# Streaming pairs of 256-token chunks as 512 columns past each weight block in a two-layer conditioned transformer block

## The reference

```
# layer 0
x = x + modulated_rms_norm(attention_16_heads(x, mask) @ Wo.T)
# layer 1, its norms with gain and bias from the condition
x = x + attention_16_heads(norm1(x)) @ Wo.T
x = x + (silu(norm2(x) @ gate_w.T) * (norm2(x) @ hid_w.T)) @ out_w.T   # 256 -> 1024 -> 256
```

## Time and profile before

| | |
|---|---|
| median of 3 runs | 324.24 us (323.45 to 324.27) |
| profiled execution: span | 321.4 us |
| its own time | not given apart from the span; the median is 2.8 us above it |
| TensorE busy | 314.3 us (98%), 5016 matmuls |
| VectorE, ScalarE, GpSimd busy | 239.0, 204.5, 182.0 us |
| transfers | 17.08 MB, mean 53 GB/s |
| mean duration of a 256-column matmul in feed-forward | 282 to 285 ns |

### The profile page before, as it was taken

One profiled execution on the slowest core, in us unless ns is written; L12 is line 12 of the kernel. 1 busy time (PEld: TensorE's weight loads), 2 busy tenths in 40 slices (PEclk: granted clock), 3 DMA queues, 4 the chain that ended last, 5 costly groups with the idle time before them and its releaser, 6 DMA issues.

```text
span 321.4 us, 11942 instructions
## 1 busy us (share of the span) xinstructions
PE 314.3 (98%) x5016; PEld 297.9 (93%) x5016; DVE 239.0 (74%) x425; ACT 204.5 (64%) x445; POOL 182.0 (57%) x207
## 2 busy tenths in 40 slices
PE   7999999999999999999999999999999999999996
PEld 7979978899999999999989999998999999999996
DVE  4995879896996987896949498898953783554344
ACT  4897687899874687587575765685462466333231
POOL 7499797244667366478742757478380653453310
PEclk9998999999999999999999999999999999999999
DMA  7955731304000300310004000100000100000001
GB/s 238 303 170 179 237 104 35 102 4 134 2 3 2 100 2 2 103 36 0 4 2 134 0 6 0 37 0 5 2 1 2 36 33 2 2 11 24 2 33 36
DMA packets 11238, 17.08 MB, mean 53 GB/s; under 512 B 1328, under 2 KB 5440, under 8 KB 11184
## 3 DMA queue, kind: packets, MB, share of 16 engines
q1 hardware_dynamic: 11008, 15.80, 15.6%
q0 software_dynamic: 176, 0.51, 0.8%
HBM read 14.14 MB, written 2.16 MB: 51 GB/s over the span
## 4 chain that ended last, share of the span: by engine, by line
PE 82%; DVE 6%; POOL 4%; issue 4%; ACT 2%; DMA 1%; SPq 0%; DVEq 0%; POOLq 0%; ACTq 0%
PE ps L1594 63%; PE ps L1709 6%; PE ps L1691 5%; PE ps L1742 3%; PE ps L1778 2%; PE ps L1727 2%; DVE probs L1148 1%; PE ps L1679 1%; DVE row_max L1140 1%; POOL x L442 1%; DMA x_T<-in_xT 1%; POOL w_lo L411 1%; POOL x_row L422 1%; DVE xs_g L1215 1%; DVE xs_row L1202 1%
## 5 line engine op out<-in xcount | busy, mean ns | idle before, releaser
L474 POOL TENSOR_TENSOR h_lo<-w_stage,h_hi 128x512 fp32r<-128x512 f32 x29 | 37.4, 1290 | 43.0 <-ACT h_hi L769 43.0
L468 POOL TENSOR_TENSOR probs<-probs,inv_row 128x512 f32<-128x512 f32 x40 | 41.3, 1050 | 34.3 <-DVE inv_row L1161 34.2
L1140 DVE TENSOR_REDUCE row_max<-ps 128x8 f32<-128x512 f32 x64 | 40.8, 681 | 9.6 <-PE ps L1691 9.4
L706 ACT ACTIVATE probs<-probs 128x512 f32<-128x512 f32 x64 | 38.8, 633 | 9.6 <-DVE probs L1148 9.3
L1234 DVE SCALAR_TENSOR_TENSOR w_stage<-w_stage,ps 128x512 f32<-128x512 f32 x32 | 21.7, 677 | 29.9 <-ACT w_stage L762 29.8
L1148 DVE SCALAR_TENSOR_TENSOR probs<-row_max,ps 128x512 f32<-128x512 f32 x64 | 41.1, 677 | 0.9 <-PE ps L1709 0.9
L1594 PE MATMUL ps<-ff_hi,w_hi 128*128 128x256 f32 x256 | 41.6, 285 | 0.0
L1594 PE MATMUL ps<-ff_lo,w_hi 128*128 128x256 f32 x256 | 40.9, 282 | 0.0
L1594 PE MATMUL ps<-ff_hi,w_lo 128*128 128x256 f32 x256 | 40.9, 282 | 0.0
L762 ACT ACTIVATE w_stage<-ps 128x512 f32<-128x512 f32 x32 | 19.1, 597 | 33.3 <-PE ps L1594 33.2
L713 ACT ACTIVATE probs_T<-ps 128x512 f32<-128x512 f32 x64 | 34.8, 603 | 7.3 <-PE ps L1709 7.0
(11 more groups left out here) (105 smaller groups left out, 721.4 us busy)
## 6 DMA issues: line engine op xcount, KB each, us to landing
w_stage<-in_weights SPq DMA_DIRECT2D x20, 256.0 KB, 4.6
mod_tile<-mod_rows_dram SPq DMA_DIRECT2D x32, 128.0 KB, 3.2
x_T<-in_xT SPq DMA_DIRECT2D x8, 256.0 KB, 3.7
x_row<-in_x SPq DMA_DIRECT2D x8, 256.0 KB, 3.0
out<-x SPq DMA_DIRECT2D x7, 256.0 KB, 2.1
x<-in_cond POOLq DMA_DIRECT2D x1, 392.0 KB, 6.5
out<-x SPq DMA_DIRECT2D x2, 128.0 KB, 2.0
x<-in_rows POOLq DMA_DIRECT2D x1, 96.0 KB, 6.7
```

The lines of the kernel that those rows point to most:

```text
L468: pool.tensor_tensor(by_head, by_head, inv_row[r][:].unsqueeze(2).to_broadcast([P, 2 * NR, S]), ALU.mult).then_inc(normed, 1)
L474: pool.tensor_tensor(h_lo[q % 2][:], h_T[q % 2], h_hi[q % 2][:], ALU.subtract)\
L706: act.activation(probs[n % NPROB][:], probs[n % NPROB][:], ACT.Exp, scale=-SCALE)\
L1140: dve.tensor_reduce(row_max[r][:], ps[:, S_BANK[a][r], :].rearrange("p (g s) -> p g s", s=S), AX.X, ALU.max).then_inc(max_ready, 1)
```

## The change

- **Keys and queries by pairs.** `KQ` lists groups of chains: 0 and 1 alone, then 2 and 3, 4 and 5 and so on. `keys(n)` and `queries(n)` make a whole group: the moving operand takes 256 tokens of each of two neighbouring slots of `in_both`, 512 columns, and each output half has a bank of its own. They wait for the split inputs of both chains. `copy_keys(a)` and `copy_queries(a)` read each chain's part of the two banks.
- **Feed-forward by pairs of chunks.** `hidden_in(p, j)` streams the 512 tokens of chunks 2p and 2p + 1 (`ff_both`, four slots instead of two); gate and hidden features have a bank each. A group q is now one block j of the pair, q = 8p + j, again 512 elements. `hidden_out(p, j)` has four token tiles and so 12 matmuls of 256 columns; it waits for group q. `hidden_hi(q)` waits for the down products of group q - 2, as before.
- **The end.** The last pair ends in four quarters, each of 128 tokens, in four banks.
- **`CHAINS`** is reordered so that the chains of a pair are neighbours. All bank tables and the lists of all five engines are new. In TensorE's list `hidden_in(0, 0)` now stands after `scores(8)` and `output_product(6)`, where it stood after `scores(6)`, `output_product(5)` and `values(8)`.
- Transfers: x_T of chunk 1 moves ahead of q0, and `store_mods` and the first two `load_rows` ahead of the h and u weight blocks. The scratch area for GpSimd's own transfers is set to 8192 bytes.

```diff
+KQ = [[0], [1], [2, 3], [4, 5], [6, 7], [8, 9], [10, 11], [12, 13], [14, 15]]
-NS = 2
+NS, NIN, NFF = 2, 2, 4
 def pair(t, lo, hi):
-    return t[:, lo:hi + 1, :]
+    return t[:, lo:hi + 1:hi - lo, :]
...
-        in_hi = slots("in_hi", NS, [P, KT, TC], F32R)
-        in_lo = slots("in_lo", NS, [P, KT, TC], F32R)
+        in_both = sb("in_both", [P, NIN, 2, KT, TC], F32R)
...
-        ff_hi = slots("ff_hi", 2, [P, KT, TC], F32R)
-        ff_lo = slots("ff_lo", 2, [P, KT, TC], F32R)
+        ff_both = sb("ff_both", [P, NFF, 2, KT, TC], F32R)
...
-                wait(act, gu_ready, NJ * (k - 1))
-                act.activation(ff_hi[k % 2][:], xs_g[a % 2][:], ACT.Copy).then_inc(ff_hi_ready, 1)
+                wait(act, gu_ready, NJ * ((k - NFF) // 2 + 1))
+                act.activation(ff_hi[k % NFF], xs_g[a % 2][:], ACT.Copy).then_inc(ff_hi_ready, 1)
...
                 act.wait_ge(h_ready, q + 1)
-                wait(act, h_used, 2 * q - 2)
+                wait(act, h_used, q - 1)
...
+            def features(name, banks, g):
+                def moving(k):
+                    at = g[0] % NIN
+                    if len(g) == 1:
+                        return in_hi[at][:, k, :], in_lo[at][:, k, :]
+                    return tuple(in_both[:, at:at + 2, part, k, :] for part in range(2))
+                def dst(m):
+                    if len(g) == 1:
+                        return ps[:, banks[0], TC * m:TC * m + TC]
+                    return ps[:, banks[m], :].rearrange("p (n s) -> p n s", n=2)
...
+            def keys(n, *readers):
+                c, l = CHAINS[KQ[n][0]]
+                blocks = features(f"k{l}", K_BANK[n], KQ[n])
...
+                pe.wait_ge(in_hi_ready, KQ[n][-1] + 1)
...
+            def hidden_in(p, j, *readers):
+                at = 2 * p % NFF
+                blocks = [(ps[:, GU_BANK[NJ * p + j][n], :].rearrange("p (n s) -> p n s", n=2),
+                           [(w_parts(name, kt, P * j, P, HID),
+                             tuple(ff_both[:, at:at + 2, part, kt, :] for part in range(2))) for kt in range(KT)], True)
+                          for n, name in enumerate(("gate", "hid"))]
...
+                pe.wait_ge(ff_hi_ready, 2 * p + 2)
+                bank_free(*readers)
+                products(blocks, BOTH_HIGH)
...
+                products(blocks, FIRST_LOW)
+                pe.wait_ge(ff_lo_ready, 2 * p + 2)
+                products(blocks, SECOND_LOW, closing=True).then_inc(gu_ready, 1)
...
+            def hidden_out(p, j, *readers):
+                q = NJ * p + j
+                blocks = [out_block(p, j, t, j == 0 and (t % 2 == 0 or 2 * p + 2 == NCH)) for t in range(2 * NT)]
```

The new list of TensorE from the last blocks of the second pair to the first of the third (after `hidden_out(1, 7)` come `weigh_values_T(11)` and `scores(13)`), and the end of the list:

```diff
+            output_product(11, acc_read(3))
+            transpose_probs(12, 0)
+            transpose_normed(10, scores_read(12, 3))
+            transpose_probs(12, 1, pT_read(12, 0, 0), scores_read(13, 0))
+            values(13, scores_read(13, 1))
+            weigh_values_T(12)
+            transpose_normed(11, xsT_read(10))
+            output_product(12)
+            transpose_probs(13, 0)
+            keys(8, y_read(12), v_read(13))
+            transpose_normed(12, pT_read(13, 0, 0))
+            queries(8, scores_read(13, 3))
+            transpose_probs(13, 1, xsT_read(12), pT_read(13, 0, 1))
+            scores(14, k_read(15))
+            weigh_values_T(13)
+            output_product(13)
+            values(14)
+            values(15, q_read(15))
+            transpose_normed(13, v_read(14))
+            scores(15, scores_read(14, 1))
+            transpose_probs(14, 0, v_read(15), xsT_read(13))
+            hidden_in(2, 0, scores_read(14, 3))
...
+            hidden_in(3, 7, gu_read(29))
+            hidden_out(3, 4)
+            hidden_out(3, 5)
             last_hidden_out(0)
             last_hidden_out(1)
+            last_hidden_out(2)
+            last_hidden_out(3)
```

More of the change, by code:

```diff
@@ L1920, in _ @@
-            hidden_in(0, 1)
-            hidden_in(0, 2, scores_read(6, 2), scores_read(6, 3))
-            hidden_in(0, 3)
-            hidden_in(0, 4, gu_read(0, 0))
-            hidden_in(0, 5)
-            hidden_out(0, 0, y_read(5))
-            scores(7, gu_read(0, 1), q_read(8), pT_read(6, 0, 0))
-            transpose_probs(6, 1, gu_read(0, 2))
+            transpose_normed(3)
+            output_product(4, v_read(6))
+            transpose_output(5)
+            transpose_probs(6, 0)
+            scores(7, v_read(7), xsT_read(3), scores_read(6, 3))
@@ new lines, in _ @@
+            output_product(5, y_read(4))
+            keys(5, pT_read(6, 0, 0))
+            queries(5, scores_read(7, 0), pT_read(6, 0, 1))
+            transpose_normed(4, y_read(5))
+            transpose_probs(6, 1, k_read(9))
+            values(8, scores_read(7, 1))
+            transpose_normed(5, scores_read(7, 2))
+            weigh_values_T(6)
+            scores(8, q_read(9), xsT_read(4))
+            transpose_probs(7, 0, scores_read(7, 3), xsT_read(5))
+            output_product(6, oT_read(6))
@@ new lines, in _ @@
+            hidden_in(0, 0, scores_read(8, 0), pT_read(7, 0, 0))
+            hidden_in(0, 1, pT_read(7, 0, 1), scores_read(8, 1))
+            hidden_in(0, 2, v_read(8), y_read(6))
+            transpose_probs(7, 1, gu_read(0))
+            hidden_in(0, 3, gu_read(1))
+            scores(9, gu_read(2), pT_read(7, 1, 1))
+            weigh_values_T(7, scores_read(8, 2))
+            transpose_probs(8, 0, gu_read(3))
+            values(9, scores_read(8, 3))
+            hidden_out(0, 0, pT_read(8, 0, 1))
@@ L1928, in _ @@
             hidden_out(0, 1)
+            hidden_in(0, 4, v_read(9), scores_read(9, 0))
+            hidden_in(0, 5, scores_read(9, 1), oT_read(7))
             hidden_out(0, 2)
[L1930 to L1935 removed]
+            transpose_probs(8, 1, gu_read(4))
@@ L1962, in _ @@
[L1962 to L1972 removed]
+            transpose_normed(6, scores_read(10, 0))
@@ new lines, in _ @@
+            transpose_probs(9, 1, scores_read(10, 1), pT_read(9, 0, 1))
+            output_product(7, acc_read(0))
+            values(10, scores_read(10, 2))
+            output_product(8, acc_read(1))
+            scores(11, xsT_read(6), scores_read(10, 3), pT_read(9, 1, 0))
+            weigh_values_T(9)
+            transpose_probs(10, 0, y_read(8), v_read(10))
+            values(11, y_read(7))
+            transpose_normed(7, pT_read(10, 0, 1))
+            transpose_probs(10, 1, scores_read(11, 0))
@@ new lines, in _ @@
+            output_product(9, oT_read(9))
+            weigh_values_T(10)
+            keys(7, scores_read(11, 1), y_read(9))
+            transpose_normed(8, scores_read(11, 2))
+            transpose_normed(9, v_read(11))
+            output_product(10)
+            values(12)
+            queries(7, xsT_read(9))
+            hidden_in(1, 0, k_read(13))
+            hidden_in(1, 1, v_read(12), scores_read(11, 3))
+            hidden_in(1, 2, gu_read(8))
+            transpose_probs(11, 0, gu_read(9))
```

1571 lines of the change are left out of this document (715 added, 856 removed), and 20 rows, old and new, of tables (GU_BANK, S_BANK, T_BANK).

## The result

The change makes the kernel slower: 356.1 us (median of 5, 352.4 to 357.7) against 324.2 us (5 runs beside them, 323.4 to 326.9), a ratio of 1.098, 95% interval 1.094 to 1.102. The profiled execution took 352.43 us (span 350.6); it is the fastest of its five, so its rows understate the loss by some 4 us. The forecast was 321.4 with a range to 329.

What follows compares the result with a forecast made beforehand. It took the time as TensorE's work plus its waits, with VectorE level before the first feed-forward work. From 324.2 us, 9.9 less work and 7.1 more waiting gave 321.4 us, range 315 to 329.

Steps and rivals of the forecast that it cites:

- 512 columns at 217 ns: Gate/hidden products, paired keys and queries: 217 ns per 512-column matmul, saving 7.8 us and 1.5 us of TensorE work.
- The bound of 237: Upper estimate for a 512-column matmul: twice 118.6 ns, 237 ns, if the surplus goes by the column.
- the rival built on it (0.08): 512-column matmuls cost 237 ns, so the change doesn't give what it says: 330.7 us, chance 0.08.
- Waits before the first pair, 1.0 (at most 2.3): Before the first paired feed-forward work: VectorE gets 11.3 us more, TensorE 9.0; 1.0 us more waiting taken.
- Second pair 0 (worst 3): Scores of chain 10 to the second pair's first block: no added wait, at worst 3 us by the chain of latencies.
- Third boundary 5.6 (0 to 8): From scores(13) to hidden_in(2, 0): 5.6 us more waiting, 2.8 of it ahead of transpose_normed(11); bounds 0 and 8.
- End 1.2: Ahead of last_hidden_out(0): hidden_hi(31) waits for group 29's down product, 0.95 us bare plus 0.24 for the low part.
- Clock: A long wait might drop TensorE to 1.2 GHz for 3.6 us, losing 1.8 us; counted within the other cases.
- the pair starves TensorE: Waiting for the second chunk costs its whole chain at each pair: 14.4 us of waits, 328.7 us, chance 0.25.

Runs made afterwards that it cites:

- experiment 11: Kernel after with 48 more TensorE instructions ahead of keys(0) and row maxima over every second score column only: 346.3 us, ratio 1.066.
- Experiment 7: Kernel after with 48 more TensorE instructions ahead of keys(0), 13 tiny matmuls replacing one warm-up matmul, same work: 350.1 us, ratio 1.079.
- experiment 1: Kernel after with in_both and ff_both laid out so a pair's 512 moving columns stand in one run of addresses: 355.9 us, ratio 1.100.
- experiment 8: Kernel after with every 512-column matmul issued as two of 256 (347.6 us), plus the third boundary's longest chain moved earlier in the order: 350.9 us.
- experiment 12: The early-chain version of experiment 8 with six x1 slots instead of five and a scratch area of 4096 instead of 8192: 346.3 us, ratio 1.070.
- experiment 4: Kernel after with extra 256-column matmuls filling the waits ahead of transpose_normed of chains 5, 11, 13 and 15: 352.4 us, ratio 1.089.
- experiment 15: Kernel before with six extra 256-column matmuls in the 0.5 us wait ahead of transpose_probs(0, 1): 323.6 us, ratio 1.0001.
- experiment 5: Kernel after with only the paired keys and queries issued as 256-column matmuls, hidden_in keeping 512: 344.5 us, ratio 1.065.
- experiment 9: Kernel before with 112 more TensorE instructions ahead of keys(0), 30 tiny matmuls replacing two warm-up ones, same work: 335.6 us, ratio 1.035.
- experiment 10: Kernel before with row maxima taken over every second column of the scores only: 320.4 us, ratio 0.990.
- experiment 14: Kernel before with 256 more TensorE instructions ahead of keys(0), 66 tiny matmuls replacing two warm-up ones: 325.1 us, ratio 1.005.
- experiment 3: Kernel after with five dense loops of 96 matmuls behind its last product, columns, layout and weights varied: 232.4 ns per 512-column matmul; total time without meaning.

## Why the prediction was wrong

- **512 columns at 217 ns.** Failed. 232 ns in the kernel, 232.4 alone. Hidden_in's 384 matmuls save 1.8 us, not 7.8, and the 168 of keys and queries (233 ns against 2 x 113) lose 1.2 where 1.5 were to be saved. The step took the mask's pair, 227 ns, as the disturbed case and the stream at 2.4 GHz as the rule. The bound of 237 was in the text, and the rival built on it (0.08) was nearly right in its mechanism: 8.5 of the 9.9 us were never there.
- **Waits before the first pair, 1.0 (at most 2.3).** Failed most: 14.9 us (24.6 against 9.7). The step compared sums of work of two engines, VectorE's 11.3 us against TensorE's 9.0. VectorE never filled (74% busy), and with less load on it (experiment 11) the stretch was 1.4 us shorter, with more stops in it. Three things stood in its place. First, stops for instruction fetches: 0.8, 0.6, 3.3 and 1.6 us beyond the spacing at 30, 42, 69 and 96 us, and 0.7 at 165: 7.0 us, where the kernel before has none. Second, half-rate stretches, 13.7 us until 78 us against 3.4: at most 5 us. Third, the rest, 3.5 us or more, waits one behind the other, of about 1 us each (transposes of the output, keys(2), the input of weigh_values(2, 0)). Experiment 7 shows that a shift of the stream alone takes part of the first two away: 20.0 us of loss there against 24.6, with 2.9 us of gaps at stops against 6.7 and half-rate stretches of 6.8 us against 13.7. The profiled execution of the kernel after is its luckiest: in the trace of experiment 1, with the same places and the usual time of 356.4 us, the gaps at stops are 10.4 us in place of 7.5 over the whole run, and the half-rate stretches are the same 20.5.
- **Second pair 0 (worst 3).** 4.9 us from the first pair's block to the second's, of it the stop of 0.7 at 165 us; the kernel before lost 7.5 in all its time after 94 us.
- **Third boundary 5.6 (0 to 8).** Place right, size wrong: 12.9 us, the longest ahead of transpose_normed(11), as forecast (2.8), and the next ahead of transpose_normed(13). The view of waits of this stretch (us in total, times, longest):
```profile
PE ps L1803 <- DVE xs_row L1218: 5.7, 2, 3.6
PE ps L1734 <- ACT probs_T L733: 1.2, 1, 1.2
PE ps L1608 <- ACT o_hi L741: 0.7, 1, 0.7
```
The chain from output_product(11) to transpose_normed(11) takes 9.6 us (234.9 to 244.5) where the step had 6.8. Two of its rows, then the wait:
```profile
235.90 0.38 ACT L755 ACTIVATE x<-ps 128x256 f32<-128x256 f32 x1 [3.11 <-DMA out<-x]
...
242.23 2.17 DVE L1218 TENSOR_SCALAR xs_row<-x,root_x 128x256 f32<-128x256 f32 x2 [0.64 <-POOL root_x L473]
...
244.46 0.66 PE L1803 MATMUL ps<-ident,xs_row 128*128 128x128 f32 x4 [3.57 <-DVE xs_row L1218]
```
The squares of y(7) start 1.0 us after their product, because chunk 7 takes its x1 slot from chunk 2, which the pairing sets free only with the pair's last product (experiments 8 and 12), and norm_x takes 2.17 us where the earlier trace rows have 1.29. The step had neither. Two half-rate stretches of 3.4 us follow the two waits (at most 3.4 us between them).
- **Before the fourth pair** the prediction had no term at all; TensorE waits 1.3 us there, ahead of transpose_normed(15) at 307.6 us.
- **End 1.2.** Right: 0.94 us ahead of last_hidden_out(0) and 0.35 for the low part.
- **Clock.** The case was named (1.8 us for a dip). It came four times, 20.5 us at 1.2 GHz against 3.4. That is at most 8.5 us; experiment 4 puts the third boundary's dips at 0.9 to 3.5 us together, experiment 15 puts one at 0 to 0.7.
- **The stops** were in no step. They were not to be seen in the trace of before, but its counts (5,016 loads, as many matmuls, 40 fetches) and its stretches of 256 small instructions in 3 us were.

So of the 30.6 us of added loss, 7.0 are stops, up to 8.5 clock, and 15 or more are waits by themselves. The rival "the pair starves TensorE" (14.4 us of waits) comes near to that last part; with the columns' rival added it gives 338 us, and 7.0 of stops and up to 8.5 of clock bring that to 353.5 at most, beside 352.4 in the profiled execution. How the waits of 15 us divide between the pairing and the new order of the chains no experiment separates; experiment 5, the fastest build that keeps the pairing and does the whole work, still stands 21 us above the kernel before, 4 us of stops included.

## What to carry to other kernels

Count instructions as well as work: a list of many small matmuls has places where 256 instructions pass in 3 us, and an edit anywhere ahead shifts which of them meet a fetch, by up to 12 us in a kernel of 324. So compare two orders at two or three shifts of the stream (a few tiny instructions at the start) before one of them is called slower. And before streaming more columns, measure the spacing at both widths: if it grows with the columns, there is little to save, and a pairing that is bought with it has to wait for nothing.

## What the runs showed of the hardware

- **TensorE stops at fixed places in its stream.** With each load, matmul and separate wait counted as one from TensorE's first record, the traces of thirteen of the kernels have 52 gaps of 0.65 us or more from start to start between neighbouring matmuls of one run with no wait between them. All 52 stand at instruction 192 or 193 past a multiple of 256 (the expectation of experiment 9 counts eight more at the start and says 201). The kernel before and experiments 10, 14 and 15 have none.
- **A stop ends with the fetch of the place before.** Paired in order, one fetch of 16 KB belongs to each such place, and all 52 stops end 2.2 to 3.1 us (median 2.4) after the fetch of the place 256 instructions earlier has started. So TensorE stops where it covers 256 instructions faster than that fetch starts and lands. In the longest stop of experiment 9 the fetch started 4.1 us behind its place, beside dense transfers, and TensorE was at the next place after 2.9. Of the 648 starts in 17 traces half lie between 0.1 us ahead and 1.8 us behind the last matmul ahead of the place (median 0.9 behind), and a tenth come more than 3.4 us behind it, up to 7.5. What sets the start stays open. The Trainium skill, "Runtime: NRT & Kernel Launch", section "Instruction fetch mechanics", has the blocks of 16 KiB and 256 instructions, and the trace agrees; it also has the cost of crossing one as mostly hidden, and there the runs disagree: up to 4.4 us from one matmul to the next at a crossing (experiment 3; 4.2 in experiment 4) where small matmuls are dense.
- **The surplus of a matmul grows with its columns:** 118.7 ns for 256 and 232.4 for 512, so 12.0 and 19.1 ns over the 106.7 and 213.3 at 2.4 GHz; at 512 whatever the layout of the moving side or the reuse of the weights.
- **A dip of the clock can cost less than its half:** the one of 3.4 us in the kernel before is worth 0 to 0.7 us, not 1.7 (experiment 15).
